# Steps unrolled as a pipeline of three, with static addresses, in a linear-attention and expert layer

## The reference, cut to what matters

```python
xn = _layernorm(x)
qkv = silu(xn @ w_qkv.T)                  # 16 heads, 128 wide each for q, k, v
# per head, in blocks, with decays that depend on the head's slope:
o_inter = (q * q_decay) @ kv
o_intra = ((q @ k.T) * diag_decay) @ v
kv = block_decay * kv + (k * k_decay).T @ v
out = norm_w * out * rsqrt(mean(out * out) + eps)      # over all 16 heads
attn = (sigmoid(xn @ w_gate.T) * out) @ w_out.T
routed = sum over the row's top 4 experts of score * (silu(xn @ wg) * (xn @ wu)) @ wd
shared = sum over 2 of (silu(xn @ swg) * (xn @ swu)) @ swd
return x + attn + routed + shared
```

## Time and profile before

| | |
|---|---|
| device time, median of 3 runs | 1897.66 us (1895.84 to 1899.8) |
| span of the profiled execution | 1961.1 us |
| own device time of the profiled execution | not given beside the profile |
| first phase / steps 0 to 15 / 16 to 63 / 64 to 127 / closing | 192.4 / 200.6 / 744.1 / 794.9 / 29.1 us |
| busy in the span: PE / DVE / ACT / POOL | 94% / 62% / 51% / 18% |

### The profile page before, as it was taken

One profiled execution on the slowest core, in us unless ns is written; L12 is line 12 of the kernel. 1 busy time (PEld: TensorE's weight loads), 2 busy tenths in 40 slices (PEclk: granted clock), 3 DMA queues, 4 the chain that ended last, 5 costly groups with the idle time before them and its releaser, 6 DMA issues.

```text
span 1961.1 us, 39254 instructions
## 1 busy us (share of the span) xinstructions
PE 1847.6 (94%) x12603; PEld 1635.2 (83%) x12603; DVE 1210.9 (62%) x2452; ACT 998.5 (51%) x1693; POOL 346.9 (18%) x375
## 2 busy tenths in 40 slices
PE   6999997999999999999999998989998989899998
PEld 6888886878888888888888888978897889788987
DVE  7888885855445455454555556665666566656665
ACT  4334443455565555665556554544454545454542
POOL 2331577720000000000000013030303030303011
PEclk9999997999999999999999999999999999999998
DMA  6665333333443434434334332020202020202014
GB/s 217 219 236 194 105 123 107 122 107 123 129 126 122 128 120 124 136 119 127 123 120 139 122 94 79 4 78 4 73 9 78 4 78 4 78 4 70 12 57 151
DMA packets 175779, 199.38 MB, mean 102 GB/s; under 512 B 19744, under 2 KB 155168, under 8 KB 175648
## 3 DMA queue, kind: packets, MB, share of 16 engines
q1 hardware_dynamic: 150944, 138.87, 22.8%
q0 software_dynamic: 12288, 33.57, 5.4%
q10 hardware_dynamic: 12416, 25.17, 3.4%
HBM read 111.54 MB, written 86.00 MB: 101 GB/s over the span
## 4 chain that ended last, share of the span: by engine, by line
PE 80%; another core or an unknown queue 6%; issue 4%; DVE 4%; ACT 3%; DMA 1%; SPq 0%; DVEq 0%; ACTq 0%
PE bank L1232 6%; PE bank L1340 6%; PE bank L1233 5%; PE bank L1321 5%; PE bank L1234 5%; PE bank L1245 5%; PE bank L1247 5%; PE bank L1246 5%; PE bank L1328 5%; PE bank L1342 5%; PE bank L1281 4%; PE bank L1290 3%; PE bank L1260 3%; PE bank L1310 3%
## 5 line engine op out<-in xcount | busy, mean ns | idle before, releaser
L1245 PE MATMUL bank<-wh,xc 128*128 128x256 f32 x1024 | 304.6, 297 | 12.9 <-issue 12.9
L1247 PE MATMUL bank<-wh,xc 128*128 128x256 f32 x1024 | 290.7, 284 | 0.9 <-issue 0.9
L1246 PE MATMUL bank<-wl,xc 128*128 128x256 f32 x1024 | 290.2, 283 | 0.3 <-issue 0.3
L719 ACT ACTIVATE o<-bank 128x512 f32<-128x512 f32 x128 | 76.6, 599 | 354.3 <-PE bank L1342 244.1
L581 POOL COPY picked<-pos 128x4 uint32 x32 | 11.3, 353 | 1274.1 <-DMA slot_y<-ys 746.3
L1232 PE MATMUL bank<-xh,wh 128*128 (+1 forms) x512 | 226.2, 442 | 9.2 <-DVE state L1047 5.7
L1245 PEld LDWEIGHTS bank<-wh,xc 128*128 128x128 f32 x1024 | 197.1, 193 | 12.9 <-issue 12.9
L1233 PE MATMUL bank<-xl,wh 128*128 (+1 forms) x512 | 207.8, 406 | 0.0
L1234 PE MATMUL bank<-xh,wl 128*128 (+1 forms) x512 | 206.9, 404 | 0.0
L1340 PE MATMUL bank<-sm,kv 128*128 128x128 f32 x1024 | 197.9, 280 | 1.3 <-DVE state L1034 0.8
L1246 PEld LDWEIGHTS bank<-wl,xc 128*128 128x128 f32 x1024 | 197.2, 193 | 1.6 <-issue 1.6
(11 more groups left out here) (176 smaller groups left out, 4071.6 us busy)
## 6 DMA issues: line engine op xcount, KB each, us to landing
slot_x<-zeros ACTq DMA_DIRECT2D x8, 3072.0 KB, 10.0
we<-wexp_in SPq DMA_DIRECT2D x192, 128.0 KB
xs<-slot_x SPq DMA_DIRECT2D x96, 256.0 KB
slot_y<-ys SPq DMA_DIRECT2D x96, 256.0 KB, 2.2
wd<-wdown_in SPq DMA_DIRECT2D x192, 64.0 KB
raw<-wqkv_in SPq DMA_DIRECT2D x17, 384.0 KB
xin<-x_rows SPq DMA_DIRECT2D x8, 512.0 KB, 4.0
xn_rows<-xn SPq DMA_DIRECT2D x8, 512.0 KB, 5.4
```

The lines of the kernel that those rows point to most:

```text
L1245: pe.matmul(dst, lh, rh, start=(k == 0), stop=False)
L1246: pe.matmul(dst, lh, rl, start=False, stop=False)
L1247: mm = pe.matmul(dst, ll, rh, start=False, stop=(k == KD - 1))
```

## The change

The loops over blocks, heads and pairs of heads are gone on all engines: every step is written out, and every address is a constant. The work runs over 131 slots (`SLOTS`): slot s projects step s, attends step s-1 and projects out step s-2. Buffers `kv`, `qp` and `state` are doubled for it. `project_kv` reads `xh` and `xl` directly, so `xc` and its copies go, as do POOL's copies of indices and DVE's copies of weights. The routing work is dealt over slots 1 to 24 in three parts a block, the weights' exponential is taken of the chosen entries alone in slot 25, the experts run in slots 26 to 73 (`EXPERT0`, `EXPERT1`), the gathered results are summed in 32 slots of 75 to 119, one tile a slot, and the closing sums of a block are made three slots after the step of the last head that they need. `project_out` uses one PSUM bank for both halves instead of two.

```diff
+SLOTS = NSTEP + 3
+ROUTE0 = 1
+EXPERT0 = ROUTE0 + 3 * NSB + 1
+EXPERT1 = EXPERT0 + NPAIR // 2
+FIRST_OUT = NSTEP - NSB
...
-                pe.wait_ge(xc_ready, 2 * i + 2)
-                pe.wait_ge(tanh_done, i)
-                project_kv(0, par).then_inc(k_mm, 1)
...
-            def load_tokens(low, b):
-                src = (xh, xl)[low][:, :, bass.ds(b * SB, SB)]
-                act.copy(xc[low][:], src).then_inc(xc_ready, 1)
...
-                pool.tensor_copy(cur_pos[r][:], at_col(pos, q * CH + r)).then_inc(idx_copied, 1)
...
+            for s in range(SLOTS):
+                experts = EXPERT0 <= s < EXPERT1
+                q0 = 2 * (s - EXPERT0)
+                projects, attends, delivers = s < NSTEP, 1 <= s <= NSTEP, 2 <= s <= NSTEP + 1
+                if projects:
+                    project_kv(s, 0)
+                if attends:
+                    scores(s - 1)
+                if experts:
+                    turn(q0)
+                if s > FIRST_OUT + 2:
+                    turn_back(s - FIRST_OUT - 3)
+                if projects:
+                    project_kv(s, 1)
+                if experts:
+                    gate_up(q0)
...
+                if attends:
+                    keys_values(s - 1)
+                if delivers:
+                    project_out(s - 2, 0)
+                if experts:
+                    down(q0)
+                if projects:
+                    project_q(s)
+                if experts:
+                    turn(q0 + 1)
+                if attends:
+                    attend(s - 1)
+                if experts:
+                    gate_up(q0 + 1)
+                if delivers:
+                    project_out(s - 2, 1)
+                if projects:
+                    project_g(s)
+                    turn_keys(s)
+                if experts:
+                    down(q0 + 1)
+                if FIRST_OUT + 2 <= s < SLOTS - 1:
+                    squares(s - FIRST_OUT - 2)
```

More of the change, by code:

```diff
@@ L450, in _ @@
             sp.wait_ge(routed, 1)
-            for r in range(2):
-                load_experts(r, r)
+            sp.wait_ge(wgt_ready, 1)
+            for q in range(2):
+                load_experts(q)
             for r in range(CH):
                 sp.wait_ge(scattered[r], 16 * TOPK * NT // CH)
[L455 to L461, removed]
@@ L503, in _ @@
+            for r in range(2):
+                sp.wait_ge(out_stored[r], 16 * NSB // 2)
         @block.gpsimd
@@ new lines, in split_high_out, with silu_kv @@
+                act.copy(wh[h % 2][:, WC:WC + D], wos[:]).then_inc(wh_ready, 1)
+            split_high_in(0)
+            split_high_out(0)
+            group(NSB - 1, False)
+            def silu_kv(i, half):
+                act.wait_ge((k_mm, v_mm)[half], i + 1)
+                if half == 0 and i >= 2:
+                    act.wait_ge(kp_ready, i - 1)
+                    act.wait_ge(o_mm, i - 1)
+                act.activation(kv[i % 2][:, 2 * half:2 * half + 2, :].rearrange("p c n -> p (c n)"), bank[half][:],
+                               ACT.Silu).then_inc((k_silu, v_silu)[half], 1)
@@ new lines, in turned, with silu_pair, result @@
+            def turned(q):
+                act.wait_ge(xsT_mm, q + 1)
+                act.copy(xsT[:].rearrange("p j k m -> p (j k m)"), bank[6][:]).then_inc(xsT_ready, 1)
+            def silu_pair(q):
+                act.wait_ge(gu_mm, q + 1)
+                act.activation(sg[F:2 * F, :], bank[7][0:F, 0:2 * P], ACT.Silu).then_inc(sg_ready, 1)
+            def result(q):
+                act.wait_ge(y_mm, q + 1)
+                act.wait_ge(y_stored[q % 2], 16 * (q // 2))
+                for j in range(2):
+                    ins = act.copy(ys[q % 2][:, j, :], bank[6 + j][:, 0:D])
+                ins.then_inc(ys_ready, 1)
@@ new lines, in update_state @@
+            def update_state(j):
+                bd = hc[j // NSB % 2][:, 2 * P + 1:2 * P + 2]
+                first, last = j % SB_PER_SEQ == 0, j % SB_PER_SEQ == SB_PER_SEQ - 1
+                dve.wait_ge(kv_mm, j + 1)
+                for c in range(CH - 1 if last else CH):
+                    new = state[j % 2][:, c + 1, :] if c < CH - 1 else state[(j + 1) % 2][:, 0, :]
+                    add = bank[3][:, ch[c]]
+                    if first and c == 0:
+                        dve.tensor_copy(new, add).then_inc(state_step, 1)
+                    else:
+                        dve.wait_ge(state_step, updates_before(j, c))
+                        dve.scalar_tensor_tensor(new, state[j % 2][:, c, :], bd, add, ALU.mult, ALU.add).then_inc(state_step, 1)
@@ L1345, in steps @@
-            def steps(h, par, par_prev, experts):
-                pe.wait_ge(w_ready, h + 1)
-                for b0 in range(0, NSB, SB_PER_SEQ):
-                    step(h * NSB + b0, b0, par, par if b0 else par_prev, experts, first=True)
-                    with pe.Fori(b0 + 1, b0 + SB_PER_SEQ - 1) as b:
-                        step(h * NSB + b, b, par, par, experts)
-                    step(h * NSB + b0 + SB_PER_SEQ - 1, b0 + SB_PER_SEQ - 1, par, par, experts, last=True)
-            def head(experts):
-                return lambda h, par: steps(h, par, 1 - par, experts)
@@ L1358, in _ @@
[L1358 to L1372 removed]
+                mm.then_inc((k_mm, v_mm)[half], 1)
@@ new lines, in down, with total_counts @@
+            def down(q):
+                pe.wait_ge(hT_ready, 2 * (q + 1))
+                for j in range(2):
+                    ps = slice(j * F, (j + 1) * F)
+                    mm = pe.matmul(bank[6 + j][:, 0:D], hT[ps, :], wd[q % 2][ps, :], start=True, stop=True)
+                mm.then_inc(y_mm, 1)
+            def total_counts():
+                pe.wait_ge(macc_ready, NSB + 1)
+                pe.matmul(bank[3][:, CH * E:CH * E + E], ones_bf[:], macc[:], start=True, stop=True).then_inc(tot_mm, 1)
```

952 lines of the change are left out of this document (418 added, 534 removed).

## The result

The changed kernel takes 1833.58 us (median of 4 runs, 1832.82 to 1835.63) where the kernel before takes 1898.73: a ratio of 0.9659, interval 0.9642 to 0.9676, 65 us less. The span of the profiled execution is 1831.1 us, the forecast for it was 1839.7; the forecast of the time was 1808, with a stated range of 1768 to 1845.

A forecast was written before the change was run, and what follows sets the result against it. PE, busy 94% of the span, was taken as the bound: 192.4 first phase + 1611.3 matmuls + 28.0 closing + 8 leftovers = 1839.7 us span, lowered to a time of 1808 us, range 1768 to 1845.

The forecast's parts named there:

- PE's work: All matmuls stay at the quiet pace: 80 plain steps 876.0 us, 48 expert steps 735.3, together 1611.3 us.
- The walk through a slot: Timing one plain 11.0 us slot: PE gets scores, attention, state and projection inputs in time and does not wait.
- The slack of the keys: Transposed keys are copied by 1.2 us into the next slot, scores start at 1.4: 0.2 us spare, the smallest.
- Rivals 2 and 4: Late keys' copy on ACT stalls scores: 2, 24 to 40 us, chance 0.10; 4, clock drops too, 1905 to 1990 us, 0.05.
- Loops gone: 128.3 us of waits and low clock go with branches and the short line (square, gate, high part, next Silu).
- Scatter later: POOL's last scatters end in slot 25, hidden before slot 26 by 5 us or so; 3 us kept as risk.
- Leftovers: 8 us stay: 2 for slot 25's exponential, 3 for the first expert pair, 3 for clock falls after these.
- Closing: 28.0 us against 29.1: 12.7 added to PE's line in slots, 15.3 from a 20 us chain after slot 127.
- The sum: Span forecast: first phase 192.4, PE's work 1611.3, closing 28.0, leftovers 8, together 1839.7 us, 121.4 less than before.
- From the span to the time: Runs' median lies 63.4 us under the profiled span; between 1780 and 1840, about the middle was taken: 1808 us.
- rival 1: The timed runs of before had few of the profiled waits: 1825 to 1845 us, at 1834; chance 0.18.
- Rival 3: Waits without a releaser stay, since straight code must be fetched too: two thirds of 128 us, 1870 to 1895; chance 0.07.

The follow-up runs named there:

- GpSimd put right: The kernel before with GpSimd's loops alone written out and its index copies gone, other engines' loops kept: 1869.00 us, ratio 0.9831.

## Why the prediction was right or wrong

**The 65 us, taken apart**, in the second and third job, where before takes 1899 to 1900:

| version | us | ratio | what went, against the one above |
|---|---|---|---|
| before | 1899.4 | 1 | |
| all loops written out | 1878.8 | 0.9887 | branches, and the low clock behind them: 20.6 us |
| and no index copies | 1855.4 | 0.9750 | scatter 24 us earlier, wait at step 16 from 39.4 to 17.8 us: 23.4 us |
| changed kernel | 1833.8 | 0.9638 | the rest of that wait, by experts from slot 26 on: 21.6 us |

The first two rows are runs against runs. The last is read from two traces: step 16 of the version above it takes 35.4 us, 20.2 over its pace (the wait of 17.8 and a granted clock of 0.71), and slots 25 and 26 of the changed kernel are 4.8 over theirs; the closing gives some 4 us more. No run moved the experts alone. Nor was before itself profiled in a job in which it takes 1899: that its time there holds the late scatter and the turns is inferred from its neighbours, whose sums meet it (1878.8 + 20 at the turns).

*PE's work*: right, and what decided. 46 slots at 10.95 us; slots 32 to 39 took 122.25 us (567.25 to 689.50) against 122.54. Reading `xh` and `xl` in place of `xc` cost nothing, as costed.

*The walk through a slot*: right, no wait above 0.25 us in the 128 projecting slots but the three named. The slack of the keys is 0.6 us where it was read, not 0.2. Rivals 2 and 4, which lived on it, did not come.

*Loops gone*: the loss in the slots did go, all but 4.8 of 128 us, and the reason was right only in part. I put all lost time down to branches and to the short line across two steps. What the runs show, in jobs where before takes 1899: branches some 20 us (before to written out, and as much at the five turns with GpSimd put right; the written-out version of that kernel is only 13.6 us faster, as its wait at step 16 is longer, 17.8 us against 15.3), the late scatter some 45 (23.4 + 21.6), the short line nothing, for the written-out old order keeps the quiet pace in steps 64 to 126. The overlap of three steps, which is the larger part of the diff, gave no time that a run here shows; what paid was that the experts start ten steps later.

*Scatter later*: I had its place right (hidden, in slot 25) and its worth wrong. In the trace of before it was not to be seen, because steps 0 to 15 were slow themselves: they took 218 us, the last scatter started at 406.8, and step 16 wanted its rows at 411.99, just when they were there. With those steps at pace it is the first thing on the path, 39 us of it. The wrong bounds hid this further: they put the loss of these steps at 25.4 us where it was 42.8. I costed the move as a risk of 3 us and not as the condition for the gain.

*Leftovers*: 8 us forecast, 4.8 measured (slot 25 took 12.89 in place of 10.8 us, slot 26 18.01 in place of 15.3). Beside the exponential (0.31 us) ScalarE has two table loads of 1.28 us, VectorE waited 5.16 us for the result, and PE waited 0.97 and 0.60; the first expert pair cost 2.49, forecast 3. The 3 us for clock falls did not come, as the granted clock stayed at 1.00.

*Closing*: 28.0 was forecast beyond the pace of the slots. From slot 120 to the end it took 119.3 us, 31.7 more than eight plain slots; but slots 0 and 1, in which fewer than three steps are in flight, were 6.3 us short of two, which makes 25.4. Behind slot 127 (1808.1) the chain takes 23.0 us against the forecast of 20.

*The sum* for the span was 8.6 us high: 3.2 by the leftovers, 2.6 by the 48 expert slots (732.7 without the loss in slot 26, against 735.3), 2.6 by the closing, 0.7 by the first phase; plain slots took 0.5 more.

*From the span to the time*: this is the step that failed. I took half of the 63.4 us between the profiled span of before and its median off. Each run has its span now, and time and span differ by 1.7 us (1832.82 and 1831.1), the time being the longer. The execution of before whose profile was shown must then have taken some 1962.8 us: by its waits it was one like those of the first job, where before takes 1941 to 1957, and slower still. So nothing was to be taken off a sum that already left the waits out: 1839.7 + 1.7 = 1841 follows from it, and 1834 came, by rival 1. It had a chance of 0.18; the forecast's own range (1775 to 1830) misses 1833.58, and the stated range holds it through that rival alone. Rival 1 in this form fits all runs: the timed runs of before had few of the waits without a releaser, and the change had 65 us to win and not 121.

The Trainium skill has a constant of 6.2 us by which a profile's total exceeds the execution time (Runtime: NRT & Kernel Launch, "The ~15us preamble/postamble breakdown"). The runs here do not show it: their time is 1.7 us longer than the span from the first to the last instruction. That the forecast with this constant, 1834, meets the result is luck, since the sum for the span was 8.6 us high.

*Rival 3* (waits without a releaser stay in straight code) is half true: in the first job they did stay, with no loop left. In the jobs where the changed kernel ran there were none to stay. The reason given for it, that straight code must be fetched too, is not borne out: those waits mostly have no packet of an instruction queue near them.

What stays open: what those waits are. They follow the job, not the chip (the written-out old order ran on one chip both times) and not the loops or copies; no row of the traces names what was waited for.

The turns are another matter. A turn of a long loop cost PE 2 to 3.6 us, and one of a two-step loop nothing that can be measured. The Trainium skill says that a taken branch whose target is not in the current two pages forces a fetch of that page before execution goes on (the same page, "Instruction fetch mechanics"); it gives no price. The trace agrees: a packet of the instruction queue is under way at each of the five turns, and at none of the short ones does PE stop.

## What to carry to other kernels

A profile is one execution: before a stall is costed, see whether the timed runs have it, by the distance of the profiled time from their median, and do the sum from the pace of quiet stretches, which held here to 1%. When all steps get faster, ask what runs beside them at its own pace (here GpSimd's scatter, some 180 to 200 us long) and will be waited for next; the cheap cure for it, indices read where they lie, was worth as much as all the loops. Check a stage's bounds by an instruction that only that stage has (here the first turn of expert rows). Test a large rewrite by its parts: the copies gone from ScalarE were worth nothing here, and no run shows a gain from the overlap.

## What the runs showed that I had not expected

- The written-out old order takes 1910 or 1879 us on the same chip in two jobs, and before 1948 or 1899. For the written-out one nearly all of it (32.8 of 33.7 us) is in steps 64 to 126, in which ScalarE has waits that no instruction of the trace explains; steps bound by PE keep their pace to 0.1 us in both jobs. In the slower job it is not even: the four runs lie between 1896 and 1915.
- 96 unused bytes a partition in SBUF ahead of other tiles shortened slots by 0.07 us plain and 0.12 with experts (15.16 against 15.28) in the mean, some 9 us in all. Nothing but the place of the tiles behind the pad was changed, so their addresses are the likely cause; which address matters, and on which engine, was not tried.
- Writing out VectorE's loops alone made the kernel 0.45% slower (interval 0.2 to 0.7%); ScalarE's alone did nothing, though its loop runs six times a head.
